# First phase: DMA transposes of bf16 parts in place of 12 of 16 TensorE transposes a batch, and new orders on every engine

## The chip, the cores and the metric

One core of a Trainium2 chip. The metric is the device time of one execution in microseconds, the median over repeated executions. The kernel before took 1605.69 us (three runs, 1605.08 to 1610.11).

## The reference, cut to what matters

The program takes 32 batches of 256 x 256 through four blocks with gated residuals. The change lies in the first block, which is the kernel's first phase:

```python
def _prob(x):
    x = jnp.tanh(x) * 0.499 + 0.5
    return jnp.clip(x / (jnp.sum(x, axis=-1, keepdims=True) + EPS), EPS)
q_prob, k_prob = _prob(q), _prob(k)             # q = _layernorm(x), k = v = ctx_1024
log_ratio = jnp.log(q_prob) - jnp.log(k_prob)
sid = jnp.einsum('bnd,bmd->bnm', q_prob - k_prob, log_ratio)
attn = jax.nn.softmax(-sid / D ** 0.5, axis=-1)
attn_feat = jnp.einsum('bnm,bmd->bnd', attn, v)
f_diff = (v - attn_feat) @ W_diff.T + b_diff + q
h = _layernorm(f_diff, ln_g, ln_b)
mlp = jax.nn.gelu(h @ W1.T + b1, approximate=False) @ W2.T + b2
x = x + jnp.tanh(g_xattn[0]) * _layernorm(mlp + f_diff, ln_g, ln_b)
```

An 8-bit product, an attention with 16 heads and a second MLP follow; they are the second phase.

## The kernel before, in words

A batch lies in SBUF as 128 partitions by two row tiles of 256 (128x512 elements). The first phase, `phase_a`, is a software pipeline of six stages. In one iteration each engine works on six batches at once, named by their lag: `n` (statistics and first layer norm `xh`), `b` (tanh, probabilities `pr`), `q` (logarithms `lg`, the differences, the context's product `U`), `u` (scores, softmax, attention, `f`), `m` (layer norm `hn`, hidden layer, gelu `G`), `w` (output product `o`, last layer norm, residual `X`). 32 batches and six stages make 37 iterations.

The order of work is written out by hand: each of the five engines has a block with its own function `iteration`, whose list of calls at the end is the order in which that engine issues. Engines meet through counting semaphores; `sig["x"]` is raised when step x is done, and `done(b, back=1)` is the count that step x has after the batch before.

A product of two f32 tiles is made of three bf16 products (`TERMS`, line 890): each operand is split into a high part (a copy in bf16) and a low part (what the copy left over). So each operand needs a high part, a low part, and its contracted axis on the partitions. Before the change the axis is turned by TensorE: `transposed` (line 903) multiplies four 128x128 blocks of an f32 tile by the identity into PSUM. Four tiles are turned in each iteration: `lr` (the log difference, of batch `u`), `df` (the probability difference, `u`), `hn` (`m`) and `E` (the exponentials, `u`). From PSUM ScalarE writes the high parts `lT`, `dT`, `hT` (lines 494 and near, the eviction of `lT` at 487) and VectorE the low parts, each from the PSUM bank and the high part (`lT` line 677, `dT` line 672, `hT` line 706).

`df` is made by GpSimd (`difference`, line 386), `lr` by VectorE (`log_difference`, line 689) from the logarithms of ScalarE (line 494). GpSimd also makes `xb` (`xh` plus a bias, line 397), `xg` (residual plus a bias, 408), `f` plus a bias (425), `ctlo` (the context's low part, 446), the inverse deviations (`vef`, `veo`, `vex`, line 352 and 354) and two of the four low parts `GT` of the gelu, whose other two are VectorE's (line 780). SP issues the loads: `xin`, `ctxn`, `mask_in`, `X`, `ctxt`.

The second phase turns two bf16 tiles by DMA, `b_nm` (128x256) and `b_y` (128x512); the first phase has no such transfer before the change.

Of the kernel before, what the change touches and what calls it, by code (L numbers as in the profile page):

```python
# [11 lines left out]
P = 128  # L12
# [143 lines left out]
def phase_a(nc, NB, x_d, ctx_d, ctxT_d, mask_d, X, mu1, rs1, top1, bottom1, masked, ident, identb, minus_half,  # L156
# [8 lines left out]
    with scope:  # L165
# [30 lines left out]
        df = two("df", [P, T, D], F32)  # L196
        lr = two("lr", [P, T, D], F32)
# [3 lines left out]
        dT = sb("dT", [P, 2, C, S], BF16)  # L201
        lT = sb("lT", [P, 2, C, S], BF16)
# [14 lines left out]
        hT = sb("hT", [P, 2, C, S], BF16)  # L217
# [17 lines left out]
        dT_ps = eT_ps = banks[0]  # L235
        lT_ps = banks[1]
        sid_ps = att_ps = banks[2]
        U_ps, mlp_ps, out_ps, hT_ps = banks[3], banks[4:6], banks[6], banks[7]
# [38 lines left out]
        def _(sp):  # L277
            def iteration(half, parity):
                b = first = lagged(half, parity, L_LOAD, NB)
                if b:  # L280
                    p, at = b.parity, bass.ds(b.number, 1)
                    if (due := done(b, back=2)) is not None:
# [3 lines left out]
                    if (due := done(b, back=2)) is not None:  # L286
# [3 lines left out]
                    if (due := done(b, back=1)) is not None:  # L290
# [3 lines left out]
                b = lagged(half, parity, L_PROB, NB)  # L294
                if b:
                    p, at = b.parity, bass.ds(b.number, 1)
                    sp.dma_start(X[:, at].rearrange("p o t d -> p (o t) d"),
                                 x_d[at].rearrange("o p t d -> p (o t) d")).then_inc(sig[f"X_in{p}"], 16)
                    if (due := done(b, back=2)) is not None:
                        sp.wait_ge(sig["U_mm"], due)  # L300
                    sp.dma_start(ctxt[p][:, :, :],
                                 ctxT_d[at].rearrange("o p c s -> p (o c) s")).then_inc(sig[f"ctxt{p}"], 16)
                if at_batch(first, 0):
# [26 lines left out]
        def _(pool):  # L330
# [34 lines left out]
            def iteration(half, parity):  # L365
# [15 lines left out]
                def difference():  # L381

                    pool.wait_ge(sig["pr"], done(q))
                    if (due := done(q, back=2)) is not None:
                        pool.wait_ge(sig["dT_mm"], due)
                    nc.gpsimd.tensor_tensor(df[q.parity][:, :, :], pr[:, 0:T, :], pr[:, T:2 * T, :],
                                            ALU.subtract).then_inc(sig["df"], 1)
# [60 lines left out]

                if m:
                    with_mlp_bias()  # L450
                if b:
                    context_low()
                if q:
                    difference()
                if w:
                    with_gated_bias()
                    output_inverse_std()
# [7 lines left out]
                if b:  # L465
                    with_bias()
# [5 lines left out]
        def _(act):  # L472
            def iteration(half, parity):
                n, b, q, u, m, w = [lagged(half, parity, lag, NB) for lag in range(6)]

                def difference_transposed():

                    act.wait_ge(sig["dT_mm"], done(u))
                    if (due := done(u, back=1)) is not None:
                        act.wait_ge(sig["sid_mm"], due)  # L480
                    nc.scalar.activation(dT[:, 0], dT_ps[:, :, :], ACT.Copy, scale=D ** -0.5).then_inc(sig["dThi"], 1)

                def logs_transposed():
                    act.wait_ge(sig["lT_mm"], done(u))
                    if (due := done(u, back=1)) is not None:
                        act.wait_ge(sig["sid_mm"], due)
                    nc.scalar.activation(lT[:, 0], lT_ps[:, :, :], ACT.Copy).then_inc(sig["lThi"], 1)
# [20 lines left out]
                def mlp_high():  # L508
                    act.wait_ge(sig["hT_mm"], done(m))
                    if (due := done(m, back=1, per=HC // 2)) is not None:  # L510
                        act.wait_ge(sig["mlp_mm"], due)
                    nc.scalar.activation(hT[:, 0], hT_ps[:, :, :], ACT.Copy).then_inc(sig["hhi"], 1)
# [28 lines left out]
                def gelu(j):  # L541
# [6 lines left out]
                    for i in range(2):  # L548
                        last = nc.scalar.activation(G[:, 2 * j + i], mlp_ps[j % 2][:, i], ACT.Gelu,  # L549
# [16 lines left out]
                def mlp_normalised():  # L566

                    act.wait_ge(sig["nmr"], done(m))
                    if (due := done(m, back=1)) is not None:
                        act.wait_ge(sig["hT_mm"], due)  # L570
# [12 lines left out]
                if u:  # L583
                    logs_transposed()
                    difference_transposed()
                load_functions(nc, act, LN_AND_EXP)
                if q:
                    logarithms()
                if m:
                    mlp_normalised()  # L590
                if q:
                    context_product()
                if m:
                    mlp_high()
                if u:
                    exponentials()
                load_functions(nc, act, GELU_AND_TANH)
                if b:
                    tanh()
                if m:  # L600
# [31 lines left out]
        def _(dve):  # L632
# [20 lines left out]
            def iteration(half, parity):  # L653
# [16 lines left out]
                def difference_low():  # L670
                    dve.wait_ge(sig["dThi"], done(u))
# [3 lines left out]
                def logs_low():  # L675
                    dve.wait_ge(sig["lThi"], done(u))
                    nc.vector.tensor_tensor(lT[:, 1], lT_ps[:, :, :], lT[:, 0], ALU.subtract).then_inc(sig["lT"], 1)
# [6 lines left out]
                def log_difference():  # L684

                    dve.wait_ge(sig["lg"], done(q))
                    if (due := done(q, back=2)) is not None:
                        dve.wait_ge(sig["lT_mm"], due)
                    nc.vector.tensor_tensor(lr[q.parity][:, :, :], lg[:, 0:T, :], lg[:, T:2 * T, :],
                                            ALU.subtract).then_inc(sig["lr"], 1)  # L690
# [99 lines left out]
                if u:  # L790
                    logs_low()
                    difference_low()
# [4 lines left out]
                if u:  # L797
                    lowest()
                if n:
                    mask_minimum()  # L800
                if m:
                    mlp_low()
                if q:
                    attention_base()
                if w:
                    output_sum()
                if u:
                    denominators()
                if b:
                    probability_factors()  # L810
                if m:
                    gelu_low(0)
                if w:
                    first_update()
                if u:
                    attention_sum()
                if m:
                    gelu_low(3)
                if w:
                    extremes()  # L820
                if at_batch(b, 0):
# [63 lines left out]
        def _(pe):  # L885
# [13 lines left out]

            def transposed(dst, src, step):  # L900
# [1222 lines left out]
```

## Time and profile before

| | |
|---|---|
| median of three runs | 1605.69 us (1605.08 to 1610.11) |
| the profiled execution, its own time | 1610.62 us |
| its span in the profile | 1608.8 us |
| busy in the span: PE (TensorE's products) | 1481.0 us, 92% |
| PEld (its weight loads, beside PE) | 1142.4 us, 71% |
| DVE (VectorE) | 1317.8 us, 82% |
| ACT (ScalarE) | 1134.1 us, 70% |
| POOL (GpSimd) | 1033.2 us, 64% |

The first phase takes about the first 604 us of the span, and its steady part, in which all six stages run, is most of it. Shares over the whole span mix two phases with different limits, so a window of the steady part is what to read. In the views, a row of a group has the source line, the engine, the operation, out<-in with the shapes, the count, the busy time, the mean duration and the idle time before it with what ended it. DMA rows give the time from issue to landing. A row of the waits says who waited for whom, with the sum, the number and the longest of those waits.

### The profile page before, as it was taken

What the parts mean: (1) busy time and instruction counts of PE and PEld (TensorE: products, weight loads), DVE (VectorE), ACT (ScalarE), POOL (GpSimd) and SP (SyncE); (2) the same over time, 40 slices, a digit from 0 to 9 for tenths busy, and PEclk for the clock granted to TensorE, in tenths of its full rate; (3) what the DMA queues carried; (4) which work ended last, traced back from release to release, by engine and by line L of the source; (5) the groups of instructions that cost most, each with busy time, mean ns of one, the idle gap of its engine ahead of it and who ended that gap; (6) DMA issues with size and microseconds to landing.
All of it is one profiled execution on the core that took longest, in us unless ns stands there. A gap on an engine that the chain in (4) does not pass through costs nothing.

```text
span 1608.8 us, 42469 instructions
## 1 busy us (share of the span) xinstructions
PE 1481.0 (92%) x14155; PEld 1142.4 (71%) x14155; DVE 1317.8 (82%) x3187; ACT 1134.1 (70%) x2057; POOL 1033.2 (64%) x1392
## 2 busy tenths in 40 slices
PE   3899999999999972677999999999999999999997
PEld 2788888888888861434677777777777777777666
DVE  3798888888888875778888889898988889898742
ACT  7898888888888742355666666676666666676664
POOL 4688888888888744324556565666656565665445
PEclk8899999999999995588999999999999999999999
DMA  7322322322222002332223232323323232322200
GB/s 227 106 72 67 96 67 66 97 65 73 90 65 72 1 1 91 81 120 77 75 77 92 72 91 80 85 80 85 87 75 90 72 96 72 87 80 84 64 17 22
DMA packets 193593, 125.42 MB, mean 78 GB/s; under 512 B 40304, under 2 KB 192752, under 8 KB 193264
## 3 DMA queue, kind: packets, MB, share of 16 engines
q1 hardware_dynamic: 193520, 124.46, 26.5%
q8 instruction: 44, 0.72, 0.2%
q14 instruction: 29, 0.24, 0.1%
HBM read 92.69 MB, written 25.17 MB: 73 GB/s over the span
## 4 chain that ended last, share of the span: by engine, by line
PE 53%; DVE 3%; issue 2%; POOL 2%; ACT 1%; DMA 1%; SPq 0%; POOLq 0%
PE b_bank L1833 31%; PE b_bank L1908 7%; PE b_score L1873 5%; PE b_scoreT L1890 4%; PE b_bank L1841 3%; PE b_bank L1985 2%; DVE b_nm L1651 1%; PE b_bank L1923 1%; ACT b_E L1469 1%; DMA b_yT<-b_y 0%; POOL b_YT L1402 0%; PE b_scoreT L1858 0%; DVE b_xh L1740 0%; DVE b_v L1714 0%; POOL b_YT L1399 0%
## 5 line engine op out<-in xcount | busy, mean ns | idle before, releaser
L1469 ACT ACTIVATE b_E<-b_scoreT 128x1024 f32<-128x1024 f32 x256 | 262.0, 1023 | 149.9 <-PE b_scoreT L1890 148.9
L1651 DVE TENSOR_REDUCE b_nm<-b_score 128x4 bf16<-128x1024 f32 x256 | 313.3, 1224 | 52.2 <-PE b_score L1873 47.0
L31 ACT ACT_TABLE_LOAD x157 | 201.4, 1283 | 19.7 <-PEq L1059 16.4
L1833 PE MATMUL b_bank<-f,b_YT 128*128 128x256 bf16 x1536 | 191.4, 275 | 4.6 <-POOL b_YT L1402 4.6
L890 PE MATMUL bank<-hT,W1T 128*128 128x256 bf16 x1536 | 183.3, 273 | 2.6 <-DVE hT L706 1.9
L1833 PE MATMUL b_bank<-b_hT,f 128*128 128x256 bf16 x1536 | 183.4, 273 | 0.8 <-DVE X L1747 0.8
L890 PE MATMUL bank<-W2T,G 128*128 128x256 bf16 x1024 | 172.7, 274 | 6.6 <-DVE GT L780 6.1
L1833 PEld LDWEIGHTS b_bank<-f,b_YT 128*128 128x128 bf16 x1536 | 144.0, 99 | 40.3 <-issue 19.5
L1833 PEld LDWEIGHTS b_bank<-b_hT,f 128*128 128x128 bf16 x1536 | 147.7, 98 | 30.3 <-issue 12.6
L890 PEld LDWEIGHTS bank<-hT,W1T 128*128 128x128 bf16 x1536 | 148.0, 98 | 27.9 <-ACT G L549 4.0
L1386 POOL TENSOR_TENSOR b_v<-b_v,b_e 128x512 f32<-128x512 f32 x32 | 40.6, 1269 | 193.5 <-DVE b_e L1732 193.5
L1402 POOL TENSOR_TENSOR b_YT<-b_Y,b_YT 128x512 bf16<-128x512 f32 x128 | 148.7, 1162 | 10.7
L1399 POOL TENSOR_SCALAR b_YT<-b_Y 128x512 bf16<-128x512 f32 x128 | 81.9, 640 | 104.1 <-ACT b_Y L1529 97.4
L890 PE MATMUL bank<-W2T,GT 128*128 128x256 bf16 x512 | 140.4, 274 | 0.0
L1529 ACT ACTIVATE b_Y<-b_bank,b1f 128x256 f32<-128x256 f32 x256 | 104.0, 472 | 51.4 <-PE b_bank L1833 51.0
L1908 PE MATMUL b_bank<-b_E,b_V 128*32 128x256 f32 x2048 | 132.5, 388 | 0.0
L1873 PE MATMUL b_score<-b_K,b_Q 48*128 48x256 bf16 x1024 | 102.6, 280 | 25.0 <-DMA b_K<-k_dram 12.5
L549 ACT ACTIVATE G<-bank,b1c 128x256 f32<-128x256 f32 x256 | 103.5, 466 | 29.7 <-PE bank L890 29.7
L890 PEld LDWEIGHTS bank<-W2T,G 128*128 128x128 bf16 x1024 | 99.0, 98 | 23.7 <-issue 12.5
L1890 PE MATMUL b_scoreT<-b_Q,b_K 49*128 49x256 bf16 x1024 | 100.8, 275 | 7.2 <-ACT b_E L1469 6.2
L1740 DVE TENSOR_SCALAR b_xh<-X,b_mv,b_rs 128x256 f32 (+1 forms) x64 | 61.8, 1005 | 43.6 <-POOL b_rs L1380 43.6
L1908 PEld LDWEIGHTS b_bank<-b_E,b_V 128*32 128x32 f32 x2048 | 57.4, 110 | 49.3 <-issue 22.5
(222 smaller groups left out, 3516.7 us busy)
## 6 DMA issues: line engine op xcount, KB each, us to landing
b_Q<-q_dram SPq DMA_DIRECT2D x192, 64.0 KB, 2.6
b_K<-k_dram SPq DMA_DIRECT2D x192, 64.0 KB, 2.9
xin<-in_x SPq DMA_DIRECT2D x32, 256.0 KB, 3.1
ctxn<-in_ctx SPq DMA_DIRECT2D x32, 256.0 KB, 2.8
mask_in<-in_mask SPq DMA_DIRECT2D x32, 256.0 KB, 3.0
X<-in_x SPq DMA_DIRECT2D x32, 256.0 KB, 4.0
ctxt<-in_ctxT SPq DMA_DIRECT2D x32, 256.0 KB, 4.2
b_ctxt<-in_ctxT SPq DMA_DIRECT2D x32, 256.0 KB, 2.9
```

The source lines that it names most:

```text
L31: act.add_instruction(mybir.InstLoadActFuncSet(name=nc.get_next_instruction_name(), act_func_set_id=which, ins=[], outs=[]))
L549: last = nc.scalar.activation(G[:, 2 * j + i], mlp_ps[j % 2][:, i], ACT.Gelu, bias=b1c[:, 2 * j + i:2 * j + i + 1])
L890: last = nc.tensor.matmul(out_tile, lhs(i, k), rhs(j, k), start=k == 0 and (i, j) == TERMS[0], stop=k == chunks[-1] and (i, j) == TERMS[-1])
L1399: nc.gpsimd.tensor_scalar(YT[:, 0, 2 * j:2 * j + 2], Y[:, 2 * j:2 * j + 2], 1.0, 0.0, ALU.mult, ALU.add).then_inc(sig["Yhi"], 1)
L1402: nc.gpsimd.tensor_tensor(YT[:, 1, 2 * j:2 * j + 2], Y[:, 2 * j:2 * j + 2], YT[:, 0, 2 * j:2 * j + 2], ALU.subtract).then_inc(sig["Ylo"], 1)
L1469: nc.scalar.activation(E[:, pair:pair + 2], scoreT_ps[:, :, :, :], ACT.Exp).then_inc(sig["E"], 1)
L1529: last = nc.scalar.activation(Y[:, 2 * j + i], bank[BANK[f"H{j}"]][:, i], ACT.Silu, bias=b1f[:, 2 * j + i:2 * j + i + 1])
L1651: nc.vector.tensor_reduce(pair, score_ps[:, :, :, :], AX.X, ALU.max, negate=True).then_inc(sig["nm"], 1)
L1833: last = nc.tensor.matmul(out_tile, lhs(i, k), rhs(j, k), start=start and k == chunks[0] and (i, j) == TERMS[0], stop=stop and k == chunks ...
L1873: last = nc.tensor.matmul(score_ps[:, odd, t], Q4[m.parity][rows, i, tile(t)], K4[m.parity][rows, i, :], start=True, stop=not mask)
L1890: last = nc.tensor.matmul(scoreT_ps[:, odd, k], K4[a.parity][rows, i, tile(k)], Q4[a.parity][rows, i, :], start=True, stop=not mask)
L1908: last = nc.tensor.matmul(bank[BANK[name]][ONE * j:ONE * (j + 1), g % 2, :], V[a.parity][:, k, i, :], E[:, i % RING, k, :], start=k == 0, ...
```

## The change

- `df` and `lr` become the two halves of one f32 tile `dl` (128x1024): GpSimd still writes the first half, VectorE the second. ScalarE copies the whole of it, scaled, to the high parts `dls[:, 0]` (`differences_high`), and VectorE writes the low parts `dls[:, 1]` from `dl` and the high parts (`differences_low`), both one stage earlier than before (batch `q` instead of `u`). One DMA on SP's queue turns the four parts, 128x2048 bf16, into `dlT`, which has two buffers; `scores` of the next iteration reads it.
- `hn` is split in the same way into `hs` (`mlp_high`, `mlp_low`), and a DMA turns it, 128x1024 bf16, into `hT`, which `hidden` reads in the same iteration.
- TensorE's transposes of `lr`, `df` and `hn` go. Of the PSUM banks that this frees one becomes a third bank for the hidden layer (`mlp_ps`), and the scores (`sid_ps`) get a bank of their own, which they shared with the attention (`att_ps`) before. The transposes of `E` stay.
- SP issues the two transposes among the loads, each behind a wait for its low part (`transpose_parts`).
- The lists of calls of all five engines are in another order.

The core of the diff:

```diff
-        df = two("df", [P, T, D], F32)
-        lr = two("lr", [P, T, D], F32)
+        dl = sb("dl", [P, 2, T, D], F32)
+        dls = sb("dls", [P, 2, 2, T, D], BF16)
...
-        dT = sb("dT", [P, 2, C, S], BF16)
-        lT = sb("lT", [P, 2, C, S], BF16)
+        dlT = two("dlT", [P, 2, 2, T, C, P], BF16)
...
-        hT = sb("hT", [P, 2, C, S], BF16)
+        hs = sb("hs", [P, 2, T, D], BF16)
+        hT = sb("hT", [P, 2, T, C, P], BF16)
...
+            def transpose_parts(b, parts, columns, ready, freed, back, per, step):
+                sp.wait_ge(sig[ready], done(b))
+                sp.sem_inc(sig[step + "_parts"], 1)
+                if (due := done(b, back=back, per=per)) is not None:
+                    sp.wait_ge(sig[freed], due)
+                sp.sem_inc(sig[step + "_ready"], 1)
+                sp.dma_start(columns, parts, transpose=True).then_inc(sig[f"{step}{b.parity}"], 16)
...
+                if n:
+                    load_normalised()
+                if m:
+                    transpose_mlp()
+                if b:
+                    load_context()
+                if n:
+                    load_mask()
+                if b:
+                    load_residual()
+                if q:
+                    transpose_differences()
...
-                    nc.gpsimd.tensor_tensor(df[q.parity][:, :, :], pr[:, 0:T, :], pr[:, T:2 * T, :],
-                                            ALU.subtract).then_inc(sig["df"], 1)
+                    nc.gpsimd.tensor_tensor(dl[:, 0], pr[:, 0:T, :], pr[:, T:2 * T, :], ALU.subtract).then_inc(sig["df"], 1)
...
-                    nc.scalar.activation(dT[:, 0], dT_ps[:, :, :], ACT.Copy, scale=D ** -0.5).then_inc(sig["dThi"], 1)
-                    nc.scalar.activation(lT[:, 0], lT_ps[:, :, :], ACT.Copy).then_inc(sig["lThi"], 1)
+                    nc.scalar.activation(dls[:, 0], dl[:, :, :, :], ACT.Copy, scale=D ** -0.25).then_inc(sig["dlhi"], 1)
...
-                    nc.scalar.activation(hT[:, 0], hT_ps[:, :, :], ACT.Copy).then_inc(sig["hhi"], 1)
+                    nc.scalar.activation(hs[:, 0], hn[:, :, :], ACT.Copy).then_inc(sig["hhi"], 1)
...
-                    nc.vector.scalar_tensor_tensor(dT[:, 1], dT_ps[:, :, :], D ** -0.5, dT[:, 0], ALU.mult,
-                                                   ALU.subtract).then_inc(sig["dT"], 1)
-                    nc.vector.tensor_tensor(lT[:, 1], lT_ps[:, :, :], lT[:, 0], ALU.subtract).then_inc(sig["lT"], 1)
+                    nc.vector.scalar_tensor_tensor(dls[:, 1], dl[:, :, :, :], D ** -0.25, dls[:, 0], ALU.mult,
+                                                   ALU.subtract).then_inc(sig["dllo"], 1)
...
-                    nc.vector.tensor_tensor(lr[q.parity][:, :, :], lg[:, 0:T, :], lg[:, T:2 * T, :],
-                                            ALU.subtract).then_inc(sig["lr"], 1)
+                    nc.vector.tensor_tensor(dl[:, 1], lg[:, 0:T, :], lg[:, T:2 * T, :], ALU.subtract).then_inc(sig["lr"], 1)
...
-                    nc.vector.tensor_tensor(hT[:, 1], hT_ps[:, :, :], hT[:, 0], ALU.subtract).then_inc(sig["hlo"], 1)
+                    nc.vector.tensor_tensor(hs[:, 1], hn[:, :, :], hs[:, 0], ALU.subtract).then_inc(sig["hlo"], 1)
...
                 if u:
-                    logs_transposed()
+                    scores()
                 if q:
                     context_product()
-                if u:
-                    difference_transposed()
                 if w:
                     output(0)
+                    output(1)
                 if u:
-                    scores()
-                if m:
-                    mlp_transposed()
-                if w:
-                    output(1)
+                    exponentials_transposed()
                 if m:
                     hidden(0)
                     hidden(1)
-                if u:
-                    exponentials_transposed()
-                if m:
                     hidden(2)
                 if u:
                     attention()
```

Two places of the new orders follow. First GpSimd in the steady part of the first phase, from the inverse deviation of `f` (`vef`, `rsf`, `nmr`) on, before:

```order
L352 TENSOR_SCALAR vef<-mvf 128x2
L354 TENSOR_TENSOR rsf<-vef,minus_half 128x2
L434 TENSOR_TENSOR nmr<-negf,rsf 128x2
L397 TENSOR_TENSOR xb<-xh,bd_all 128x256 x2
L352 TENSOR_SCALAR ve<-mv 128x2
L354 TENSOR_TENSOR rs<-ve,minus_half 128x2
L425 TENSOR_TENSOR f<-f,b_all 128x256 x2
L446 TENSOR_TENSOR ctlo<-ctxt 128x512
L386 TENSOR_TENSOR df<-pr 128x512
L408 TENSOR_TENSOR xg<-X,gb_all 128x256 x2
```

The same engine and place in the changed kernel (its lines are numbered anew; `dl` is what was `df`):

```order
L389 TENSOR_SCALAR vef<-mvf 128x2
L391 TENSOR_TENSOR rsf<-vef,minus_half 128x2
L470 TENSOR_TENSOR nmr<-negf,rsf 128x2
L389 TENSOR_SCALAR ve<-mv 128x2
L391 TENSOR_TENSOR rs<-ve,minus_half 128x2
L444 TENSOR_TENSOR xg<-X,gb_all 128x256 x2
L423 TENSOR_TENSOR dl<-pr 128x512
L433 TENSOR_TENSOR xb<-xh,bd_all 128x256 x2
L461 TENSOR_TENSOR f<-f,b_all 128x256 x2
L389 TENSOR_SCALAR veo<-mvo 128x2
L391 TENSOR_TENSOR rso<-veo,minus_half 128x2
L482 TENSOR_TENSOR ctlo<-ctxt 128x512
```

`xg`, the difference, `xb` and `f` now stand in a row without a short piece between them, and `ctlo` comes behind the output's inverse deviation (`veo`, `rso`), which stood after `xg` before. In both kernels `vex`, `rsx`, `xh` and two `GT` follow.

Then VectorE in the steady part, from the start of its list on, before:

```order
L677 TENSOR_TENSOR lT<-bank,lT 128x512
L672 SCALAR_TENSOR_TENSOR dT<-bank,dT 128x512
L689 TENSOR_TENSOR lr<-lg 128x512
L640 BN_STATS stx<-xin 128x6 x2
L636 MEMSET dve_fence 128x1
L645 BN_AGGR mvx<-stx 128x2 x2
L650 TENSOR_REDUCE negx<-mvx 128x2
L682 TENSOR_REDUCE low<-bank 128x2
L701 TENSOR_REDUCE masked<-mask_in 128x1
L706 TENSOR_TENSOR hT<-bank,hT 128x512
L711 TENSOR_TENSOR base<-bank,xb 128x512
L718 TENSOR_TENSOR o<-bank,f 128x512
```

And in the changed kernel:

```order
L708 TENSOR_REDUCE low<-bank 128x2
L731 TENSOR_TENSOR hs<-hn,hs 128x512
L715 TENSOR_TENSOR dl<-lg 128x512
L670 BN_STATS stx<-xin 128x6 x2
L666 MEMSET dve_fence 128x1
L675 BN_AGGR mvx<-stx 128x2 x2
L680 TENSOR_REDUCE negx<-mvx 128x2
L719 RECIPROCAL rden<-den 128x2
L721 TENSOR_SCALAR nrden<-rden 128x2
L702 SCALAR_TENSOR_TENSOR dls<-dl,dls 128x1024
L743 TENSOR_TENSOR o<-bank,f 128x512
```

The three low parts that read a bank are gone; `hs` low stands right ahead of the log difference, and `dls` low between the denominators (`rden`, `nrden`) and the output's sum `o`. The mask's minimum and `base` have moved towards the end of the list.

## Rows read from the trace of the kernel before

**Rows 1.** Windows: us, busy of PE, PEld, DVE, ACT, POOL (instructions), PEclk, DMA, GB/s.

```profile
200.00:500.00 300.00, 297.37 (x2539) 260.58 (x2538) 267.59 (x841) 264.36 (x594) 261.48 (x369) 1.00 0.25 75
700.00:800.00 100.00, 80.76 (x799) 53.21 (x799) 81.64 (x154) 58.87 (x87) 45.05 (x58) 0.90 0.32 93
```

**Rows 2.** Timeline, GpSimd, 304 to 322 us: start, duration, instruction [idle before <-releaser].

```profile
304.34 0.70 POOL L352 TENSOR_SCALAR vef<-mvf 128x2 f32<-128x2 f32 x1 [1.21 <-DVE mvf L645]
...
306.12 1.43 POOL L397 TENSOR_TENSOR xb<-xh,bd_all 128x256 f32<-128x256 f32 x2
...
310.50 1.03 POOL L446 TENSOR_TENSOR ctlo<-ctxt 128x512 bf16<-128x512 f32 x1
311.50 1.26 POOL L386 TENSOR_TENSOR df<-pr 128x512 f32<-128x512 f32 x1
312.73 1.42 POOL L408 TENSOR_TENSOR xg<-X,gb_all 128x256 f32<-128x256 f32 x2
...
321.15 0.70 POOL L352 TENSOR_SCALAR vef<-mvf 128x2 f32<-128x2 f32 x1 [0.67 <-DVE mvf L645]
```

**Rows 3.** Waits, 200 to 500 us: us in total, times, longest.

```profile
POOL vef L352 <- DVE mvf L645: 16.9, 18, 1.2
...
DVE lr L689 <- ACT lg L494: 12.7, 18, 0.9
...
DVE tot L726 <- ACT th L537: 2.3, 8, 0.3
```

**Rows 4.** Timeline, weight loads of TensorE, 302 to 318 us.

```profile
302.42 0.47 PEld L903 LDWEIGHTS bank<-ident,lr 128*128 128x128 f32 x4
302.85 0.21 PEld L890 LDWEIGHTS bank<-WdS,ctxt 128*128 128x128 bf16 x2
...
311.98 2.61 PEld L890 LDWEIGHTS bank<-hT,W1T 128*128 128x128 bf16 x24
...
316.39 1.60 PEld L897 LDWEIGHTS bank<-U,eT 128*128 128x128 f32 x8
```

**Rows 5.** Groups by form, ScalarE, 200 to 500 us.

```profile
L572 ACT ACTIVATE hn<-f,nmr,rsf 128x256 f32<-128x256 f32 x36 | 19.4, 586 | 0.0
...
L494 ACT ACTIVATE lg<-pr 128x1024 f32<-128x1024 f32 x18 | 19.0, 1057 | 0.2
...
L487 ACT ACTIVATE lT<-bank 128x512 bf16<-128x512 f32 x18 | 10.8, 598 | 0.0
```

**Rows 6.** Timeline, VectorE, 302 to 308 us.

```profile
302.19 0.88 DVE L771 SCALAR_TENSOR_TENSOR f<-bank,nrden,base 128x256 f32<-128x256 f32 x2
...
306.06 0.68 DVE L677 TENSOR_TENSOR lT<-bank,lT 128x512 bf16<-128x512 f32 x1
306.66 0.69 DVE L672 SCALAR_TENSOR_TENSOR dT<-bank,dT 128x512 bf16<-128x512 f32 x1
307.91 0.69 DVE L689 TENSOR_TENSOR lr<-lg 128x512 f32<-128x512 f32 x1 [0.56 <-ACT lg L494]
```

**Rows 7.** Timelines of GpSimd and VectorE, at 27 and at 544 us.

```profile
27.27 1.04 POOL L446 TENSOR_TENSOR ctlo<-ctxt 128x512 bf16<-128x512 f32 x1 [2.38 <-DMA ctxt<-in_ctxT]
...
27.47 1.39 DVE L689 TENSOR_TENSOR lr<-lg 128x512 f32<-128x512 f32 x1 [1.56 <-ACT lg L494]
...
544.07 1.83 DVE L852 SCALAR_TENSOR_TENSOR wqkvo<-raw,wqkvo 128x512 bf16<-128x512 f32 x2
...
544.11 2.38 POOL L397 TENSOR_TENSOR xb<-xh,bd_all 128x256 f32<-128x256 f32 x2
```

**Rows 8.** Tile `lr`, its VectorE instruction: shortest, median, longest in ns, first and last start.

```profile
L689 DVE TENSOR_TENSOR lr<-lg x32: 676/692/1392, 16.5 to 547.0; 128x512 f32<-128x512 f32 x32
```

**Rows 9.** DMA issues of the transposing kind: count, median us to landing.

```profile
b_yT<-b_y SPq DMA_TRANSPOSE x32, 2.8
...
b_nmT<-b_nm SPq DMA_TRANSPOSE x32, 2.4
```

**Rows 10.** Waits of SP's own queue, 200 to 500 us.

```profile
SPq L288 <- ACT th L537: 213.2, 17, 12.6
```

More of the change, by code:

```diff
@@ L277, in _, with load_normalised @@
         def _(sp):
-            def iteration(half, parity):
[L279 to L282, printed above, removed]
+            def transpose_parts(b, parts, columns, ready, freed, back, per, step):
[5 more added lines that the diff above has]
+                sp.dma_start(columns, parts, transpose=True).then_inc(sig[f"{step}{b.parity}"], 16)
+            def iteration(half, parity):
+                n, b, q, u, m, w = [lagged(half, parity, lag, NB) for lag in range(6)]
+                first = n
+                def load_normalised():
+                    p, at = n.parity, bass.ds(n.number, 1)
+                    if (due := done(n, back=2)) is not None:
                         sp.wait_ge(sig["xh"], due)
@@ L447, in context_low @@
                                             ALU.subtract).then_inc(sig["ctlo"], 1)
+                if w:
+                    with_gated_bias()
+                if q:
+                    difference()
+                if b:
+                    with_bias()
                 if m:
                     with_mlp_bias()
+                if w:
+                    output_inverse_std()
                 if b:
                     context_low()
-                if q:
-                    difference()
-                if w:
-                    with_gated_bias()
-                    output_inverse_std()
                 if n:
@@ L508, in mlp_high @@
                 def mlp_high():
-                    act.wait_ge(sig["hT_mm"], done(m))
-                    if (due := done(m, back=1, per=HC // 2)) is not None:
-                        act.wait_ge(sig["mlp_mm"], due)
-                    nc.scalar.activation(hT[:, 0], hT_ps[:, :, :], ACT.Copy).then_inc(sig["hhi"], 1)
+                    act.wait_ge(sig["hn"], done(m))
+                    if (due := landed(m, back=1)) is not None:
+                        act.wait_ge(sig[f"hT{1 - m.parity}"], due)
+                    nc.scalar.activation(hs[:, 0], hn[:, :, :], ACT.Copy).then_inc(sig["hhi"], 1)
                 def context_product():
@@ L548, in gelu @@
                     for i in range(2):
-                        last = nc.scalar.activation(G[:, 2 * j + i], mlp_ps[j % 2][:, i], ACT.Gelu,
+                        last = nc.scalar.activation(G[:, 2 * j + i], mlp_ps[j % 3][:, i], ACT.Gelu,
                                                     bias=b1c[:, 2 * j + i:2 * j + i + 1])
@@ L797, in iteration @@
                 if u:
-                    lowest()
-                if n:
-                    mask_minimum()
+                    denominators()
+                if q:
+                    differences_low()
+                if w:
+                    output_sum()
+                if b:
+                    probability_factors()
+                if w:
+                    first_update()
                 if m:
-                    mlp_low()
+                    gelu_low(0)
+                if u:
+                    attention_sum()
                 if q:
                     attention_base()
[L805 to L816, printed above, removed]
                 if m:
@@ L820, in iteration @@
                     extremes()
+                if n:
+                    mask_minimum()
                 if at_batch(b, 0):
@@ L911, in hidden @@
                     if j == 0:
-                        pe.wait_ge(sig["hlo"], done(m))
-                    if (due := done(m, per=HC // 2, part=j + 1 - 2)) is not None:
+                        pe.wait_ge(sig[f"hT{m.parity}"], landed(m))
+                    if (due := done(m, per=HC // 2, part=j + 1 - (3 if j > 2 else 1 if j == 0 else 4))) is not None:
                         pe.wait_ge(sig["G"], due)
@@ L916, in hidden @@
                         h = 2 * j + i
-                        last = product(mlp_ps[j % 2][:, i], lambda s, k: W1T[:, s, k, h * P:(h + 1) * P],
-                                       lambda s, k: hT[:, s, k], range(C))
+                        last = product(by_rows(mlp_ps[j % 3][:, i]), lambda s, k: W1T[:, s, k, h * P:(h + 1) * P],
+                                       lambda s, k: hT[:, s, :, k, :], range(C))
                     last.then_inc(sig["mlp_mm"], 1)
@@ L979, in exponentials_transposed @@
                 def exponentials_transposed():
+                    if at_batch(u, 0):
+                        pe.wait_ge(sig["ident"], 3)
                     pe.wait_ge(sig["E"], done(u))
+                    if (due := done(u, back=1)) is not None:
+                        pe.wait_ge(sig["eT"], due)
                     transposed(eT_ps, E, "eT_mm")
@@ L986, in attention @@
                     pe.wait_ge(sig["U"], done(u))
+                    if (due := done(u, back=1)) is not None:
+                        pe.wait_ge(sig["f"], due)
                     for t in range(T):
```

112 lines of the change are left out of this document (48 added, 64 removed).

## Prediction, made before the changed kernel ran

> **What bounds the kernel now.** I read the windows first, then the waits, then the timelines of single engines. The kernel has two phases one after the other, and the change touches only the first; the second I carry over as it is. In 200 to 500 us, the steady part of the first phase, the window shows TensorE busy 297 of 300 us, VectorE 268, ScalarE 264, GpSimd 261, at a granted clock of 1.00 [rows 1]. From one start of `vef` on GpSimd to the next, 304.34 to 321.15, an iteration takes 16.81 us [rows 2], so the window holds 300/16.81 = 17.85 of them. TensorE is the bound, but not by much. The waits say how far the others are behind: VectorE waited for others 12.7 + 2.3 us in its two largest waits, 0.84 per iteration, and GpSimd 16.9 in its largest, 0.95 [rows 3]. So an iteration holds 16.81 - 0.84 = 15.97 us of VectorE's own time (its short internal gaps included) and 15.86 of GpSimd's. Of the 37 iterations of the phase (32 batches, six stages), those numbered 5 to 31 run all six stages, 27 of them; I count the change on these and nothing on the others.
>
> **TensorE.** Four transposes cost it 0.43 us of its row of work: the weight loads for `lr` start at 302.42 and those of the next product at 302.85 [rows 4]. Three such groups go: 1.29 us, and 16.81 - 1.29 = 15.52 us are left. Alone that would be worth 1.29 * 27 = 35 us, if nothing else took 15.5 us or more.
>
> **ScalarE.** It loses three evictions of 598 ns and gains one copy as wide as the logarithm's 128x1024 (1057 ns) and one of 128x512, for which I take the eviction's 598 [rows 5]. That is 1.79 out and 1.66 in; an upper bound for the second is two pieces like `hn` at 586, 1.17, so 2.23 in. With 264 of 300 us busy, 14.8 an iteration, it stays under 15.3 and ends nothing. The third bank for `mlp_ps` only loosens TensorE's wait for a gelu.
>
> **VectorE.** Three low parts leave. In a run without waits one takes 0.60 us from start to start (`lT` 306.06, `dT` 306.66) [rows 6], so 1.80. Two enter. The low part of `hs` is 512 wide with both inputs in SBUF, like `lr`, whose 0.69 is the `lT` row's 0.68 plus 0.01: 0.61. That of `dls` is 1024 wide and has no row. It costs between 0.61 (if width were free) and 1.22 (twice that); I take 1.14, twice less one start-up of 0.08 (what `lr` in its 0.61 may hold beside its columns), near the upper end, because ScalarE's rows too grow with width, 598 to 1057 [rows 5]. Own time after: 15.97 - 1.80 + 0.61 + 1.14 = 15.92. On busy time alone the change would thus stop at VectorE, not at TensorE.
>
> **The turns between VectorE and GpSimd** decide. The three low parts that leave read PSUM and one SBUF tile, and run undisturbed beside GpSimd: `lT` took 0.68 us beside `xb` at 1.43 for two, both their usual length [rows 2, 6]. The two that enter read two SBUF tiles, as `lr` does. Beside such a piece the trace shows the two engines taking turns. In the ramp GpSimd began `ctlo` at 27.27 and held it to 28.31; `lr`, begun at 27.47, took 1.39 us instead of 0.69 and ended 0.55 after `ctlo` [rows 7, 6]. At 544 us two VectorE pieces of that kind beside the two of `xb` took 1.83 us and 2.38, where 1.22 and 1.43 are usual: VectorE, GpSimd, VectorE, GpSimd, each waiting out the other's whole instruction [rows 7, 2]. In the steady part of before this costs VectorE nothing (`lr` has a median of 692 ns and a maximum of 1392 [rows 8]); by its order its two-tile pieces there meet GpSimd's short pieces, or find it waiting as before `vef`.
>
> The new orders remove that alignment. GpSimd now runs `xg`, `dl` (the old `df`), `xb` and `f` (shaped like `xb`) in one unbroken stretch, 1.42 + 1.26 + 1.43 + 1.43 = 5.5 us of wide pieces, and in that stretch VectorE has `hs` low, the log difference and `dls` low. I price the turns, in us per iteration. `hs` low meets a piece of `xg` (0.71) at a random moment: half, 0.36. The log difference stands directly behind `hs` low, and by then `dl` has queued up: nearly the whole 1.26, so 1.2. `dls` low meets a piece of `xb` or `f`: half of 0.71, 0.35. The first `GT` meets `xh` or GpSimd's own `GT`, as wide as `ctlo` (1.03): half, 0.5. The four pieces of the update meet `ctlo`, the statistics and `xh`: 0.3. The last `GT` meets the statistics as before: 0. Sum 2.7. The bounds: 0, if everything again meets short pieces, and 0.71 + 1.26 + 0.71 + 1.03 + 1.6 = 5.3, if each waits out whole pieces. I take 2.7, since only the wait of the log difference is nearly a whole one.
>
> The Trainium skill has a rule for this: its page "SBUF — State Buffer", section "Who interferes with whom", says that a VectorE instruction with two SBUF inputs contends with a GpSimd instruction that reads SBUF, and that who issues first keeps the shared ports for the whole instruction. It speaks against this change. The rows of the ramp and at 544 us agree with it; by the steady rows alone, in which VectorE is never late, only GpSimd would pay, and the sum would be the second rival's.
>
> **DMA and SP.** A transposing DMA of 128x256 bf16 (64 KB) lands after 2.4 us, one of 128x512 after 2.8 [rows 9]. That is 0.4 us for 64 KB more, so `hT` (256 KB) lands in about 3.6 and `dlT` (512 KB) in 5.2. Bounds: 2.8 for both, the larger one seen, and four and eight times 2.4, should each 64 KB be paid anew, 9.6 and 19; I take the line through the two rows, because their step is so far below a whole 2.4. `hT` is covered by `output`, 48 products of 0.109 us (24 take 2.61 [rows 4]), and the transposes of `E` that TensorE has in front of `hidden`; TensorE's slack of 3 us covers the rest. `dlT` is read only by the next iteration's scores. On SP, `ctxt`, `mask` and `X` now stand behind the wait for `hs` low, and the next `xin` and `ctxn` behind that for `dls` low. SP waited up to 12.6 us for `th` before `ctxn` [rows 10], so the loads have room, and I cost this at nothing; without that cover a late load would stand in front of `ctlo` or the statistics, and an iteration would grow by its lateness.
>
> **Sum.** VectorE 15.92 + 2.7 = 18.62 us an iteration, against TensorE's 15.52. GpSimd, at 15.86 plus 0.53 for each 512 columns of the new pieces (1.6; `ctlo`'s end to `lr`'s, 0.55, is such a piece [rows 7]), stays at 17.46. So 18.62 - 16.81 = +1.81 us, times 27 = +48.9 us. The profiled execution took 1610.62 us and would take 1659.5; the median of before is 1605.69, 4.9 lower, so the forecast is **1654.6 us**. TensorE falls to 83% busy; in 700 to 800 us, at 81%, its granted clock was 0.90 on average, between the levels 2.4 and 1.2 GHz [rows 1]. At 0.90 its 15.52 become 17.2, still hidden.
>
> **Rivals.** 0.3%, 4.8 us, is about what can be told from no change.
> (1) The turns don't fall, and it gets faster: the new orders again put the two-tile pieces beside short ones. For it: the median of `lr` [rows 8]. Against it: the unbroken stretch above. Then VectorE's 15.92 bounds: -0.89 * 27 = -24.0, 1581.7 us. It decides from the point where the turns cost less than 0.89 us an iteration. Chance 0.13.
> (2) Only GpSimd gives way. Then it is the bound at 17.46: +0.65 * 27 = +17.6, 1623.2 us. For it: `lr`'s median stays at 692 in the steady part. Against it: `lr` at 1.39. Chance 0.11.
> (3) `hT` comes late. The loop is three `hidden` (3.92), `attention` (1.60), `f` and its statistics to `vef` (302.19 to 304.34, 2.15), on to `xb` (306.12, 1.78), `hn` 1.17, `hs` high 0.60 and low 0.69, the landing: 11.9 plus the landing [rows 2, 4, 5, 6]. At 3.6 that is 15.5; it decides only above 6.7. At 8 us, 19.9: +3.1 * 27 = +83.7, 1689.4 us. Chance 0.03.
> (4) Gain and turns cancel: within 4.8 us of 1605.7. Chance 0.05.
> The forecast has 0.68; its own range is 1633 (turns of 1.9) to 1679 (turns of 3.6).
>
> **Numbers.** Slower: 0.68 + 0.11 + 0.03 = 0.82. The same 0.05, faster 0.13. The range reaches from 1604, which leaves out the first rival, to 1679, which leaves out the third; with the tails about 0.18 is outside.
>
> **What would show it.** In the changed profile: the log difference into `dl` at well over 1 us instead of 0.69, and the first `GT` on VectorE over 0.7; wide pieces of GpSimd lengthened too; an iteration of about 18.6 us; TensorE about 83% busy, waiting for `base`, and VectorE without waits. It is wrong if VectorE's two-tile pieces stay at 0.69 us and the iteration is under 16.8, if GpSimd is never idle while VectorE waits, or if TensorE's longest wait is for the landing of `hT`.

## The result, and the profile after

The changed kernel took 1674.71 us (1672.61 to 1677.46), the kernel before 1607.32 us in the same comparison. The ratio is 1.0419 (95% interval 1.0393 to 1.0446): slower by 67 us, where 1654.6 had been forecast, 49 above.

The loss lies in the first phase. The residual's update of the last stage, `X`, brackets it. Its group by tile, before and after (shortest/median/longest in ns, first and last start):

```profile
L749 DVE SCALAR_TENSOR_TENSOR X<-o,rso,xg x64: 478/485/600, 77.0 to 601.4; 128x256 f32 x48, 128x256 f32<-128x256 f32 x16
```

```profile
L774 DVE SCALAR_TENSOR_TENSOR X<-o,rso,xg x64: 470/480/1198, 79.9 to 669.4; 128x256 f32 x48, 128x256 f32<-128x256 f32 x16
```

From the first `X` to the last it is 524.4 us before and 589.5 after, 65 more, in 31 intervals. By the starts of `X` in the timeline the 26 between iterations that run all six stages average 17.10 us before and 19.40 after (+2.30, 60 us together), and the five in which the pipeline drains add another 5; the way to the first `X` adds 3. What is left of the span is the second phase's, 1007 us before and 1001 after; the profiles of the experiments scatter between 1001 and 1006 there.

The steady window after, which answers to [rows 1] (the same columns):

```profile
200.00:500.00 300.00, 254.78 (x2045) 216.69 (x2043) 278.55 (x723) 228.59 (x506) 248.04 (x327) 0.94 0.43 105
```

TensorE fell from 297 to 255 us, ScalarE from 264 to 229, GpSimd from 261 to 248, and VectorE rose from 268 to 279, although there are fewer iterations. The waits of the same window, which answer to [rows 3], say who is late:

```profile
ACT hn L604 <- POOL nmr L470: 48.9, 16, 3.6
PE bank L914 <- DVE base L736: 41.8, 16, 3.2
POOL veo L389 <- DVE mvo L675: 39.3, 15, 3.0
...
DVE X L774 <- DVE o L765: 6.3, 15, 0.5
DVE hs L731 <- ACT hs L544: 6.1, 16, 0.4
...
PE bank L914 <- DMA hT<-hs: 3.4, 5, 0.7
```

TensorE and GpSimd wait for VectorE, 2.6 us at a time; VectorE waits for others 0.4 us at a time. ScalarE waits longest, for GpSimd's `nmr`, but all that VectorE then waits for ScalarE is the 0.4 us ahead of `hs`. The landing of `hT` ends hardly any wait. TensorE's granted clock fell from 1.00, the upper of its two levels, to a mean of 0.94 in this window; that is not the loss, since TensorE waits for VectorE, and a wait of VectorE for TensorE does not reach the list, whose smallest row is 2.2 us of 300. What made VectorE longer stands in its groups (count | busy us, mean ns | idle before):

```profile
L715 DVE TENSOR_TENSOR dl<-lg 128x512 f32<-128x512 f32 x16 | 28.1, 1754 | 0.0
L702 DVE SCALAR_TENSOR_TENSOR dls<-dl,dls 128x1024 bf16<-128x1024 f32 x15 | 25.5, 1703 | 0.0
L805 DVE TENSOR_TENSOR GT<-G 128x512 bf16<-128x512 f32 x32 | 22.2, 695 | 0.0
L774 DVE SCALAR_TENSOR_TENSOR X<-o,rso,xg 128x256 f32 x30 | 21.5, 755 | 6.3 <-DVE o L765 6.3
L731 DVE TENSOR_TENSOR hs<-hn,hs 128x512 bf16<-128x512 f32 x16 | 18.5, 1154 | 6.1 <-ACT hs L544 6.1
...
L721 DVE TENSOR_SCALAR nrden<-rden 128x2 f32<-128x2 f32 x15 | 11.4, 758 | 0.5
```

The log difference takes 1754 ns, where the same instruction took a median of 692 in [rows 8]. The profile puts no idle time in front of it: a wait for the other engine is counted as the instruction's own duration. One iteration in the timelines of GpSimd and then VectorE shows the turns:

```profile
302.97 1.42 POOL L444 TENSOR_TENSOR xg<-X,gb_all 128x256 f32<-128x256 f32 x2
304.36 1.71 POOL L423 TENSOR_TENSOR dl<-pr 128x512 f32<-128x512 f32 x1
306.03 1.88 POOL L433 TENSOR_TENSOR xb<-xh,bd_all 128x256 f32<-128x256 f32 x2
307.87 2.46 POOL L461 TENSOR_TENSOR f<-f,b_all 128x256 f32<-128x256 f32 x2
```

```profile
303.75 1.20 DVE L731 TENSOR_TENSOR hs<-hn,hs 128x512 bf16<-128x512 f32 x1 [0.34 <-ACT hs L544]
304.86 1.75 DVE L715 TENSOR_TENSOR dl<-lg 128x512 f32<-128x512 f32 x1
...
308.53 1.21 DVE L702 SCALAR_TENSOR_TENSOR dls<-dl,dls 128x1024 bf16<-128x1024 f32 x1
309.67 0.68 DVE L743 TENSOR_TENSOR o<-bank,f 128x512 f32<-128x512 f32 x1
```

`hs` low starts at 303.75 inside `xg` and ends at 304.95, 0.56 after `xg`'s 304.39: it ran when `xg` was through. GpSimd's `dl`, started at 304.36, takes 1.71 instead of 1.26 [rows 2] and ends at 306.07: it waited for `hs` low first. VectorE's `dl`, started at 304.86, ends at 306.61, 0.54 after GpSimd's. Then `xb` has waited in turn, 1.88 instead of 1.43 [rows 2]. Here `dls` low got through first, and `f` paid (2.46 for two pieces as wide as those of `xb`); in most iterations it was the other way round (12 of the 15 `dls` low in the window took 1.82 or 1.83 us, three 1.21).

### The profile page after: what moved, and what is told of

Its sections match the earlier page's. It is cut to its first block, busy times and chain, and to the rows that moved or that the text cites. A ratio compares the mean times of both kernels' runs of the same rounds, so it can differ in the third digit from the quotient of the medians.

```text
span 1670.8 us, 41906 instructions
## 1 busy us (share of the span) xinstructions
PE 1466.1 (88%) x13771; PEld 1115.7 (67%) x13771; DVE 1398.7 (84%) x3155; ACT 1130.8 (68%) x2025; POOL 1067.6 (64%) x1392
## 4 chain that ended last, share of the span: by engine, by line
PE 51%; DVE 3%; issue 2%; POOL 2%; ACT 1%; SPq 0%; DMA 0%; POOLq 0%
PE b_bank L1836 31%; PE b_bank L1911 7%; PE b_score L1876 4%; PE b_scoreT L1893 4%; PE b_bank L1844 3%; PE b_bank L1988 2%; DVE b_nm L1654 1%; PE b_bank L1926 1%; ACT b_E L1472 0%; POOL b_YT L1405 0%; DVE b_xh L1743 0%; DVE b_v L1717 0%; POOL b_YT L1402 0%; POOL b_v L1389 0%; POOL b_K L1458 0%
## 5 line engine op out<-in xcount | busy, mean ns | idle before, releaser
L914 PE MATMUL bank<-W2T,G 128*128 128x256 bf16 x1024 | 184.1, 287 | 3.3 <-DVE GT L805 3.3
L914 PE MATMUL bank<-W2T,GT 128*128 128x256 bf16 x512 | 145.6, 284 | 0.0
L914 PE MATMUL bank<-WdS,ctxt 128*128 128x256 bf16 x256 | 61.1, 341 | 87.3 <-DVE base L736 71.6
L914 PEld LDWEIGHTS bank<-W2T,G 128*128 128x128 bf16 x1024 | 106.2, 104 | 21.7 <-issue 3.9
```

Of the source, the lines that this page charges most:

```text
L914: last = nc.tensor.matmul(out_tile, lhs(i, k), rhs(j, k), start=k == 0 and (i, j) == TERMS[0], stop=k == chunks[-1] and (i, j) == TERMS[-1])
```

## The experiments

The theory: an instruction of VectorE with two SBUF operands and an instruction of GpSimd wait out each other, whole, and the new orders put wide ones side by side. Rival A: the traffic of the two DMA transposes lengthens VectorE's instructions (the DMA share rose from 0.25 to 0.43). Rival B: the loop from `base` over TensorE's context and output products to `o` sets the end.

**e1: GpSimd's bias pieces cut short.**

```diff
-  tensor_tensor(xb[p][:, t, :], xh[p][:, t, :], bd_all[:, :], ALU.add)
+  tensor_tensor(xb[p][:, t, 0:16], xh[p][:, t, 0:16], bd_all[:, 0:16], ALU.add)      # xg, f alike
```

The other columns of `xb` and `xg` stay zero, and those of `f` go without their bias: the run is for the time alone.

> The changed kernel, but GpSimd's three additions of a bias row (xg, xb, f) cover 16 of 256 columns; the other columns go without their bias (left out of the computation). GpSimd is not the bound in the changed kernel (it waits 2.6 us an iteration for mvo), so its own saving is worth nothing. Theory (VectorE's instructions with two SBUF operands and GpSimd's wait out each other's whole instruction): the wide pieces beside the log difference and beside dls low are gone; the log difference falls from 1.75 to about 0.7 to 0.9 us, dls low from 1.70 to about 1.2, hs low and X stay; an iteration falls from 19.3 to about 17.6 us and the time from 1675 to about 1624 us (1612 to 1640). Rival A (the traffic of the transposing DMAs lengthens VectorE's instructions): those stay at 1.75 and 1.70, time within 10 us of 1675. Rival B (the loop over TensorE, base to context product to output to o, sets the end): VectorE's instructions may shorten, but the time stays above 1660.

Measured: 1619.97 us, ratio to before 1.0074 (1.0052 to 1.0096), 55 us less than the changed kernel. VectorE's groups, then GpSimd's:

```profile
L734 DVE TENSOR_TENSOR hs<-hn,hs 128x512 bf16<-128x512 f32 x17 | 23.6, 1387 | 6.4 <-ACT hs L547 6.4
L705 DVE SCALAR_TENSOR_TENSOR dls<-dl,dls 128x1024 bf16<-128x1024 f32 x17 | 20.7, 1219 | 0.0
...
L718 DVE TENSOR_TENSOR dl<-lg 128x512 f32<-128x512 f32 x17 | 11.9, 701 | 0.0
...
L724 DVE TENSOR_SCALAR nrden<-rden 128x2 f32<-128x2 f32 x17 | 2.9, 170 | 0.6
```

```profile
L436 POOL TENSOR_TENSOR xb<-xh,bd_all 128x16 f32<-128x16 f32 x34 | 22.0, 666 | 0.0
...
L447 POOL TENSOR_TENSOR xg<-X,gb_all 128x16 f32<-128x16 f32 x34 | 6.7, 218 | 0.2
L464 POOL TENSOR_TENSOR f<-f,b_all 128x16 f32<-128x16 f32 x34 | 6.7, 216 | 0.0
```

The log difference is back at 701 ns and `dls` low at 1219, while the DMAs move more than in the changed kernel (123 GB/s in the window against 105). `hs` low is longer, since it now meets GpSimd's `dl`. And the turns show from the other side: pieces of the same 16 columns take 218, 216 and 666 ns on GpSimd, and the long one is `xb`, which stands beside `hs` low and the log difference.

**e10: the same cut in the kernel before**, the control.

> The control of e1: the same cut (xg, xb and f get their bias in 16 of 256 columns, the rest is left out) in the kernel before. Theory: VectorE's wide pieces there hardly meet these three, TensorE is the bound, so 1605 us, within 6 of before; what e1 gained is then the change's own loss. If GpSimd's width costs in any kernel: 30 us or more less, under 1580.

Measured: 1605.89 us, ratio 0.9977 (0.9963 to 0.9991). So the width of these pieces costs 55 us in the new order and at most 3 in the old. Even of the 3 its profile shows nothing: the full iterations last 17.08 us (17.10 in the kernel before), and the last `X` starts later, at 604.1 us instead of 601.4.

**e4: the kernel before, with the two transposing DMAs added.**

```diff
+  sp.dma_start(sc2T[:, :, :], W1T[:, 0, 0], transpose=True)            # 128x1024, each iteration
+  sp.dma_start(sc4T[:, :, :], W1T[:, 0].rearrange("p c h -> p (c h)"), transpose=True)      # 128x2048
```

> The kernel before, with two transposing DMAs of the same sizes added to SP's list in each iteration (128x1024 and 128x2048 bf16, from the weights W1T into tiles that nobody reads). Theory: no engine waits for them and VectorE's instructions keep their length (lr 692 ns): 1607 us, within 6. Rival A: if the traffic makes VectorE's instructions longer by as much as the changed kernel shows (3 us an iteration), 1607 plus 40 to 90; half of that would still be 20 or more.

Measured: 1609.98 us, ratio 1.0004 (0.9991 to 1.0016). In the window the DMA share is 0.53, more than in the changed kernel, and every engine is as busy as in [rows 1]; the log difference `lr` stays at 693 ns:

```profile
200.00:500.00 300.00, 297.24 (x2538) 260.43 (x2536) 267.60 (x841) 264.52 (x594) 261.60 (x369) 1.00 0.53 122
```

Rival A falls. (These two DMAs have no reader and no wait for an engine, so the run speaks of traffic, not of a late landing.)

**e2 and e3: the changed kernel in other orders.** e2 reorders GpSimd's list alone; e3 GpSimd's and VectorE's. Of the lists' 11 and 15 calls only the places differ.

```diff
 GpSimd:  xg, difference, xb, f, output's deviation, ctlo, first norm, GT 2, GT 1, deviation of f, second
+e2:      difference, f, xb, xg, output's deviation, first norm, GT 1, ctlo, deviation of f, GT 2, second
+e3:      difference, f, xb, xg, output's deviation, first norm, GT 2, ctlo, GT 1, deviation of f, second
 VectorE: ... denominators, dls low, o, factors, update, GT 0, f, base, GT 3, extremes, mask
+e3:      ... denominators, o, dls low, factors, update, f, base, GT 0, GT 3, mask, extremes
```

> The changed kernel with another order of GpSimd's list alone (difference, f plus bias, xb, xg, output's deviation, first norm, GT 1, ctlo, deviation of f, GT 2, second deviation). Same instructions, same DMAs. Theory: the meetings shift; hs low and the update X meet short pieces, the log difference still meets a wide one: about 1 us an iteration less, 1645 us (1635 to 1660). Rival A and rival B: no change of over 10 us from 1675.

> The changed kernel with GpSimd's and VectorE's lists in another order (VectorE: low, hs low, log difference, first statistics, denominators, o, dls low, factors, update, f, base, GT 0, GT 3, mask, extremes). Same instructions, same DMAs. Theory: about 2.1 us an iteration of the waits go, and the time comes to about 1612 us (1600 to 1630); the log difference at 1.2 to 1.4, X at its usual 0.48 a piece. Rival A: within 15 us of 1675, since the traffic is the same. Rival B: VectorE's order also shortens the way from base to o, so this run alone doesn't tell it from the theory; with e1 it does.

Measured: e2 1652.27 us, ratio 1.0259 (1.0240 to 1.0279); e3 1610.54 us, ratio 1.0011 (0.9996 to 1.0026). With the same instructions and the same DMAs, 64 us of the 67 go by order alone. In e3 `X` and `dls` low have their short lengths again and the other two are shorter than in the changed kernel, though not undisturbed (the log difference 1181 ns, `hs` low 867). GpSimd pays instead, which costs nothing there (`f` 1178 ns a piece, 726 in the kernel before):

```profile
L702 DVE SCALAR_TENSOR_TENSOR dls<-dl,dls 128x1024 bf16<-128x1024 f32 x18 | 21.5, 1193 | 0.0
L715 DVE TENSOR_TENSOR dl<-lg 128x512 f32<-128x512 f32 x18 | 21.3, 1181 | 0.0
L774 DVE SCALAR_TENSOR_TENSOR X<-o,rso,xg 128x256 f32 x36 | 15.9, 482 | 3.5 <-DVE o L765 2.1
...
L731 DVE TENSOR_TENSOR hs<-hn,hs 128x512 bf16<-128x512 f32 x18 | 15.6, 867 | 0.0
```

```profile
L461 POOL TENSOR_TENSOR f<-f,b_all 128x256 f32<-128x256 f32 x36 | 41.7, 1178 | 0.0
```

VectorE is busy 285.85 of 300 us in e3. At 16.79 us an iteration that is 16.0 us and 0.8 idle, where the changed kernel has 18.0 and 1.4. So about 2.0 of the 2.6 us that an iteration gains are shorter pieces; the other 0.6 are idle time, and there e3 can't tell the theory from rival B, as was said before it ran.

e2's time fell into its range, but not in the way expected. `hs` low, which was to meet a short piece, now met GpSimd's difference and rose from 1154 to 1702 ns:

```profile
L731 DVE TENSOR_TENSOR hs<-hn,hs 128x512 bf16<-128x512 f32 x16 | 27.2, 1702 | 0.0
```

The log difference (1211 ns) and the two pieces of `X` (482 each) gained twice that. So e2 shows that the order moves the turns about, not that they could be forecast one by one.

**e5: the kernel before with GpSimd's list in the changed kernel's order.**

> The kernel before, with GpSimd's list alone in the order of the changed kernel (xg, difference, xb, f, output's deviation, ctlo, first norm, GT 2, GT 1, deviation of f, second deviation). No DMA transposes, TensorE's transposes as before. Theory: the low parts of before read PSUM and don't meet GpSimd, so only the log difference, X and z can; some of them now meet wide pieces: 0.3 to 0.5 us an iteration, 1619 us (1612 to 1630). Rival A (DMA traffic): 1608, unchanged. Rival C (GpSimd's new order is bad by itself, without the new low parts): most of the 67 us, over 1645.

Measured: 1622.24 us, ratio 1.0079 (1.0054 to 1.0104). GpSimd's new order alone is a fifth of the loss; the rest takes VectorE's new pieces, in the changed kernel's order, beside it. The timeline shows which of VectorE's pieces can meet it. Beside GpSimd's unbroken difference, `xb` and `f` (300.51 to 304.52) VectorE reads a bank or a single tile, and all keep their length:

```profile
300.51 1.26 POOL L386 TENSOR_TENSOR df<-pr 128x512 f32<-128x512 f32 x1
301.74 1.41 POOL L397 TENSOR_TENSOR xb<-xh,bd_all 128x256 f32<-128x256 f32 x2
303.12 1.40 POOL L425 TENSOR_TENSOR f<-f,b_all 128x256 f32<-128x256 f32 x2
```

```profile
301.60 0.68 DVE L702 TENSOR_REDUCE masked<-mask_in 128x512 int32 x1
302.19 0.68 DVE L707 TENSOR_TENSOR hT<-bank,hT 128x512 bf16<-128x512 f32 x1
302.79 0.68 DVE L712 TENSOR_TENSOR base<-bank,xb 128x512 f32<-128x512 f32 x1
...
307.12 1.66 DVE L741 SCALAR_TENSOR_TENSOR o<-o,mvo,gg_all 128x256 f32<-128x256 f32 x2
```

The last row, two SBUF operands beside `ctlo`, takes 1.66 us instead of 0.87. The log difference, which stands beside `xg` there, rose to a mean of 1102 ns:

```profile
L690 DVE TENSOR_TENSOR lr<-lg 128x512 f32<-128x512 f32 x17 | 18.7, 1102 | 1.1
```

**e6, e7 and e9: less to meet.** e6 takes the orders of e3 and moves the addition of `b2` from GpSimd to TensorE; e7 also gives GpSimd the log difference; e9 is e7 with another form of the addition.

```diff
-  nc.gpsimd.tensor_tensor(f[...], f[...], b2_all[:, :], ALU.add)
+  nc.tensor.matmul(out_ps[:, t], ones2, b2_parts, start=True, stop=False)     # e6, e7: 2 rows, ahead of the products
+  nc.tensor.matmul(out_ps[:, t], ones2, b2_parts, start=False, stop=True)     # e9: 128 rows, behind them
...
-  nc.vector.tensor_tensor(dl[:, 1], lg[:, 0:T, :], lg[:, T:2 * T, :], ALU.subtract)
+  nc.gpsimd.tensor_tensor(dl[:, 1], lg[:, 0:T, :], lg[:, T:2 * T, :], ALU.subtract)   # e7, e9
```

> The orders of e3, and GpSimd's addition of b2 to f (two wide pieces) is taken out: TensorE adds b2 to the output product, with one more product of two rows for each of its two row tiles. Theory: one wide piece less for VectorE to meet and 1.4 us less on GpSimd, 0.2 us more on TensorE: 0.3 us an iteration under e3, 1600 us (1592 to 1608). If VectorE's waits no longer cost anything in e3, 1610 as e3.

> As e6, and GpSimd also makes the log difference, right behind the probability difference, so that these two never meet; VectorE has one piece of two SBUF operands less. Theory: VectorE saves its 0.6 us and the turn of about 0.5 us, GpSimd gets the 1.26 us that it lost with the bias; half a us an iteration under e6: 1594 us (1585 to 1602), faster than both kernels. If GpSimd then is the bound: 1605 or more.

> As e7, but the two extra products that add b2 have the same shape as the others (128 rows, all but two of them zero) and stand behind the output's products instead of ahead of them. In e7 the row of such a product and the gap around it cost about 0.3 us each on TensorE, and TensorE stood on the path (VectorE's o waited 26 us of 300 for it), and the first output product waited 4.1 us for the parts of b2. If that is all: 0.4 us an iteration and some 3 us at the start less, 16.5 us an iteration, 1603 us (1597 to 1609). If the loop base, context product, output, o is bound by something else: 1617 to 1622, as e7.

Measured: e6 1619.52 us (ratio 1.0061, 1.0040 to 1.0083), e7 1620.11 (1.0072, 1.0052 to 1.0091): missed by 19 and 26 us. In e6 `xb` took the place of `f` beside VectorE (1183 ns a piece), so VectorE gained nothing. In e7 VectorE did become shorter, 260 us of 300, and then waited for TensorE:

```profile
DVE o L730 <- PE bank L908: 26.0, 18, 1.8
```

This points to rival B: once most of the turns are gone, the loop over TensorE is what is left, and the two small products made it longer. (TensorE is busy 290 of the 300 us there and itself waits for `base` for 9.6, so a loop through TensorE and a TensorE that is simply full come to nearly the same; no run parts the two.) The first output product also waited 4.1 us for the parts of `b2`, and the first `X` came at 85.9 us instead of e3's 77.9. e9 mends both in part (its first `X` comes at 82.3 us) and came out at 1606.39 us, ratio 0.9977 (0.9965 to 0.9989), inside the range expected: the only version here that keeps the DMA transposes and is faster than the kernel before, by 0.2%, and by 4% than the changed one. The profiles do not show where the 0.2% comes from. The steady iteration is shorter (16.56 us, before 17.06), but the first `X` is late, the next four intervals are longer (18.5 us on average, 17.3 before), and the last `X` starts at 603.0 us, where it was 601.4 before: the first phase as a whole gained nothing. VectorE's wait for TensorE is still its largest there, 19.2 us of 300.

**e8: the kernel before, in orders meant to have fewer turns.**

> The kernel before with GpSimd's and VectorE's lists in another order (same instructions; the bias pieces xb stand later, base ahead of hT low, the mask's minimum later). Theory: the few turns of before and the waits of TensorE for o and GT go: 0.4 us an iteration, TensorE bound at 16.5: 1596 us (1590 to 1604). If before has no turns worth anything: 1608.

Measured: 1611.78 us, ratio 1.0019 (1.0008 to 1.0031). It missed. `X` fell from 510 to 481 ns a piece, but the meeting moved to the gelu's low parts, which took a mean of 692 ns on VectorE in the kernel before, and TensorE now waits for them (group and wait):

```profile
L781 DVE TENSOR_TENSOR GT<-G 128x512 bf16<-128x512 f32 x36 | 35.3, 981 | 0.0
```

```profile
PE bank L891 <- DVE GT L781: 7.2, 18, 0.4
```

## Why the prediction was right

**Direction and mechanism: right.** TensorE, ScalarE and the landings behave as worked out: TensorE is 85% busy (83 forecast) and waits for `base`; its 254.78/300 * 19.40 = 16.5 us an iteration are, by an estimate, the forecast 15.52 at the mean granted clock of 0.94; `hT` lands in 3.1 us and `dlT` in 4.3 (3.6 and 5.2 forecast), both hidden. The cost sits in the turns, on VectorE, as e1, e2, e3 and e10 show, and DMA traffic has no part in it (e4). The steady rows of before alone would have said that only GpSimd pays; the rows of the ramp and the Trainium skill's rule (page "SBUF — State Buffer", section "Who interferes with whom") spoke for turns on both sides. The trace of after agrees with the rule, VectorE's log difference at 1754 ns.

**Rivals.** "The turns don't fall" would have been seen in `dl` at 0.69; it was 1.75. "Only GpSimd gives way" is refuted by the same row. "`hT` comes late" had 3.4 us of waits in 300. "Gain and turns cancel" is refuted by the 67 us. Rival B, which the prediction did not have, is hidden here; the waits of e7 point to it when most turns are taken away.

**The size: two terms of the sum were too small.** The sum had +1.81 us an iteration, times 27, 49 us. Measured: +2.30 in the full iterations, 60 us, and 8 us in the ramp and the draining, on which nothing was counted.

- The turns, forecast at 2.7 us. From the mean durations after, each less its undisturbed one (0.69, 1.22 from e1, 0.48 a piece, 0.17):

| piece | forecast | measured |
|---|---|---|
| log difference | 1.2 | 1.75 - 0.69 = 1.06 |
| `hs` low | 0.36 | 1.15 - 0.69 = 0.46 |
| `dls` low | 0.35 | 1.70 - 1.22 = 0.48 |
| first `GT` | 0.5 | 0 |
| four pieces of the update | 0.3 | 2 x (0.755 - 0.48) = 0.55 |
| `nrden`, one operand of 128x2 | none | 0.76 - 0.17 = 0.59 |
| sum | 2.7 | 3.1 |

That the sum came this near is partly luck: the 0.5 of the first `GT` did not come (it took 0.71 us, the last one 0.68), and `nrden`, which cost 0.59, was not in it.

- The waits. VectorE's 0.84 us were taken as gone. They are, but its idle time only fell from (300 - 267.6)/300 * 17.10 = 1.85 us an iteration to (300 - 278.6)/300 * 19.40 = 1.39, by 0.46: it now waits 0.4 for ScalarE's high part of `hs` and 0.4 ahead of `X`, so the sign "VectorE without waits" did not come. Turns and waits were thus 0.8 too small together, more than the 0.5 that was missed. VectorE's busy time rose from 15.25 to 18.01 us an iteration, 2.76, where the sum had 2.65; what is neither turn nor wait came out 0.3 cheaper than priced, and which pieces hold that was not taken apart.
- The 27 iterations. VectorE's new pieces meet GpSimd's in the draining iterations too, and those five got 1 us longer on average.
- The undisturbed `dls` low, which had no row, was priced at 1.14 from start to start. Its row in e1 is 1219 ns, less the 0.08 by which rows of this engine overlap: 1.14. This price held.

A slip without weight: the 16.81 us of an iteration before was the shorter of two that alternate (16.82 and 17.30 from `vef` to `vef`); the mean in the window is 17.06. It moves both sides of the difference alike, and it is a part of why 18.62 was forecast and 19.40 found.

## What to carry to other kernels

Before a VectorE instruction that reads PSUM is replaced by one that reads two SBUF tiles, look at what GpSimd does at that moment: the price is not the instruction's own time but the whole GpSimd piece beside it, and the profile shows it as a longer duration, not as a wait. Compare the mean of the same form of instruction with its shortest; where the two differ, order is what to change first, and here order alone was worth 64 us. When the turns are gone, look for what they hid before expecting the rest.

## What was not expected

An instruction with a single operand of two columns, `nrden`, also waited: 758 ns after, 169 in the kernel before and 170 in e1. Reductions and statistics with one SBUF operand did not: `masked` took 0.68 us beside the difference and `xb` in e5's rows, as in the kernel before (676 ns), and `stx`, which stands beside `xb` in the changed kernel, 409 ns (415 before). The same section of the Trainium skill lists `tensor_scalar` among the operations that may take the shared ports and says that `tensor_reduce` cannot; the rows of `nrden` and `masked` agree with both.

A product of 2 rows by 256 columns, put ahead of products of 128 rows, cost TensorE more than one of full height behind them. TensorE is busy 280.7 of 300 us in e3, 290.0 in e7 and 286.6 in e9; with iterations of 16.79, 16.90 and 16.56 us that is 15.71, 16.34 and 15.82 us an iteration. Two products of 2 rows thus took 0.6 us, two of 128 rows 0.1. Whether the height or the place does it was not tried.
